# Quantised attention: who rounds the queries and keys of batches 2 to 7, and when

## What is computed

```python
def fake_quant(x, bits=8):
    qmax = 2.0 ** (bits - 1) - 1.0
    scale = jnp.maximum(jnp.max(jnp.abs(x)) / qmax, 1e-08)
    return jnp.clip(jnp.round(x / scale), -qmax - 1.0, qmax) * scale

qkv = fake_quant(x) @ fake_quant(w_qkv) + b_qkv
q, k, v = split_heads(qkv)                      # 12 heads of 16
attn = jnp.einsum('bhnd,bhmd->bhnm', fake_quant(q), fake_quant(k)) * scale
attn = fake_quant(jax.nn.softmax(attn, axis=-1))
out = jnp.einsum('bhnm,bhmd->bhnd', attn, fake_quant(v))
out = fake_quant(out) @ fake_quant(w_proj) + b_proj
```

## Time and profile before

| | us |
|---|---|
| median of 3 runs | 2291.52 (2283.61 to 2294.26) |
| the profiled execution, its own time | 2287.18 |
| its span, first to last instruction | 2285.4 |
| the rounding block, from the first to the last of its instructions | 819.2 to 853.7 |
| the first pass, first matmul to last exponential | 859.7 to 1118.5 |

### The profile page before, as it was taken

One profiled execution on the slowest core, in us unless ns is written; L12 is line 12 of the kernel. 1 busy time (PEld: TensorE's weight loads), 2 busy tenths in 40 slices (PEclk: granted clock), 3 DMA queues, 4 the chain that ended last, 5 costly groups with the idle time before them and its releaser, 6 DMA issues. The chain is left out here.

```text
span 2285.4 us, 30890 instructions
## 1 busy us (share of the span) xinstructions
PE 1875.7 (82%) x9852; PEld 972.1 (43%) x9876; DVE 1410.9 (62%) x2476; ACT 1140.9 (50%) x2071; POOL 458.9 (20%) x626
## 2 busy tenths in 40 slices
PE   5798899698875517777488877999899998999998
PEld 4644555354334201000122244442134334888887
DVE  6555255451105678999778887999788984223222
ACT  2044245341103759999799964332477770222222
POOL 6000000001211011222100013331024443333333
PEclk9989999777875755555599978996699999999999
DMA  3011111066991006432100009777788724676674
GB/s 89 14 55 65 60 33 35 5 249 237 410 411 50 0 4 197 133 106 95 33 29 28 28 16 151 125 125 105 81 98 114 109 56 141 171 212 200 199 211 105
DMA packets 153845, 262.04 MB, mean 115 GB/s; under 512 B 28640, under 2 KB 124497, under 8 KB 148726
## 3 DMA queue, kind: packets, MB, share of 16 engines
q1 hardware_dynamic: 135366, 242.23, 39.9%
q0 software_dynamic: 18256, 18.19, 4.0%
q10 hardware_dynamic: 96, 0.01, 0.0%
HBM read 217.80 MB, written 58.76 MB: 121 GB/s over the span
## 5 line engine op out<-in xcount | busy, mean ns | idle before, releaser
L1802 PE MATMUL ps<-arena 128*128 x376 | 194.8, 621 | 108.0 <-ACT ps L1844 60.2
L1844 ACT ACTIVATE ps<-ps,arena 128x512 f32<-128x512 f32 x384 | 256.6, 1120 | 6.4 <-POOL arena L1828 6.4
L1812 DVE TENSOR_REDUCE arena<-ps 128x1024 f32 x192 | 232.7, 1224 | 24.3 <-PE ps L1802 11.9
L1844 ACT ACTIVATION_READ_ACCUMULATOR ps<-ps,arena 128x1 f32 x384 | 234.7, 668 | 0.0
L2218 DVE TENSOR_REDUCE arena<-ps 128x1024 f32 x192 | 221.7, 1216 | 8.6 <-PE ps L2463 5.7
L2719 ACT ACTIVATE arena<-ps 128x1024 f32<-128x1024 f32 x192 | 185.3, 1021 | 77.1 <-PE ps L2571 75.4
L3060 ACT ACTIVATE arena<-ps,arena 128x256 f32<-128x256 f32 x234 | 89.5, 481 | 268.4 <-PE ps L3022 268.4
L2009 ACT ACTIVATE arena<-ps 128x1024 f32<-128x1024 f32 x192 | 178.7, 1048 | 7.9 <-DVE arena L2029 4.6
L2463 PE MATMUL ps<-arena 96*128 96x512 bf16 x500 | 164.0, 433 | 21.9 <-DVE arena L2218 12.1
L3091 DVE SCALAR_TENSOR_TENSOR arena<-ps,arena 128x192 f32<-128x192 f32 x78 | 29.0, 412 | 233.1 <-issue 233.1
L2992 POOL DMA_INDIRECT out_dram<-arena x78 | 121.3, 1555 | 238.1 <-DVE arena L3091 162.1
(11 more groups left out here) (413 smaller groups left out, 3347.8 us busy)
## 6 DMA issues: line engine op xcount, KB each, us to landing
arena<-in_sm_w_dram SPq DMA_DIRECT2D x128, 576.0 KB, 15.5
arena<-in_re_w_dram SPq DMA_DIRECT2D x39, 1252.0 KB, 5.8
arena<-ra_parts SPq DMA_DIRECT2D x192, 192.0 KB, 9.0
routed_in<-routed_in SPq DMA_DIRECT2D x8, 3332.0 KB, 13.6
ra_parts<-arena SPq DMA_DIRECT2D x48, 192.0 KB, 2.4
arena<-la_xt SPq DMA_DIRECT2D x16, 512.0 KB, 3.6
arena<-routed_in SPq DMA_DIRECT2D x39, 196.0 KB, 5.4
arena<-arena SPq DMA_DIRECT2D x64, 96.0 KB, 2.2
```

The source lines that it names most:

```text
L1802: ins = pe.matmul(ps[:, 2 * (n % 4) + t % 2, :], QM[j][:, h, t * P:(t + 1) * P], KI[:, b, h // HG, :], start=True, stop=True)
L1812: v.tensor_reduce(MXq[:, b, 2 * u:2 * u + 2, at_head(h)], ps[:, 2 * (n % 4):2 * (n % 4) + 2, :], AX.X, ALU.max).then_inc(s_lk, 1)
L1844: ins = act.activation(bank, bank, ACT.Exp, bias=nb[n % 4][:, t % 2:t % 2 + 1], scale=c_reg, accum_out=RS[:, b, t, at_head(h):at_head(h) + 1])
```

## The change

The loop over all batches in the rounding block goes; its body stays for batches 0 and 1, written out. The queries and keys of batches 2 to 7 are rounded by GpSimd within the first pass: in batch b it works on batch b+2, cut into 12 pieces of 128x512 (3 that scale and 3 that subtract, for the queries and then for the keys), one ahead of each odd unit's bias. In the last two batches, which have no b+2, it does the values of batches 0 and 1 instead, which neither ScalarE nor VectorE now touches: at units 3 and 9 a scaling of 128x384, at units 15 and 21 a memset and a subtraction of 128x384. SP waits for the rounded queries of a batch before it spreads them, TensorE for its rounded keys. `TA` are the two scratch tiles: the old `TMP` and one new.

```diff
         @block.scalar
             act.wait_ge(s_one, 16 * HG)
-            with act.Fori(0, B // 2) as i:
-                for n, (j, src, bias, k) in enumerate(((0, QF, magic, 0), (0, KF, magic_k, 1), (1, QF, magic, 0))):
...
-            rq.wait(act, B // 2, 0)
-            for b in range(2):
...
+            for n, (j, src, bias, k) in enumerate(((0, QF, magic, 0), (0, KF, magic_k, 1), (1, QF, magic, 0))):
+                if n == 2:
+                    rq.wait(act, 0, 1)
...
         @block.sync
                             sp.wait_ge(s_qz, 2)
+                            rounded[0].wait(sp, b, 3)
         @block.tensor
                     sg[j].wait(pe, i, 16 * HG)
+                    rounded[1].wait(pe, b, 3)
...
         @block.gpsimd
             nbs.start(pool)
+            for k in range(2):
+                pool.sem_inc(rounded[k].sem, 6)
+
+            def part(b, k, step):
+
+                some = slice(step % 3 * S, step % 3 * S + S)
+                if step < 3:
+                    if b > 2:
+                        rounded[k].wait(pool, b - 1, 3)
+                    pool.tensor_scalar(TA[k][:, some], scaled((QF, KF)[k], b)[:, some], inv2[:, k:k + 1],
+                                       (magic, magic_k)[k], ALU.mult, ALU.add).then_inc(scl_[k].sem, 1)
+                else:
+                    scl_[k].wait(pool, b - 2, 3)
+                    pool.tensor_scalar(scaled((QI, KI)[k], b)[:, some], TA[k][:, some], MAGIC, None,
+                                       ALU.subtract).then_inc(rounded[k].sem, 1)
+            def values(b, step):
+
+                heads = T * NH // 2
+                some = slice(step % 2 * heads * HD, (step % 2 + 1) * heads * HD)
...
+                if step < 2:
+                    if step == 0:
+                        rounded[b].wait(pool, B - 1, 3)
+                    pool.tensor_scalar(at, VF[:, b, :, :].rearrange("p t d -> p (t d)")[:, some], inv2[:, 2:3], magic,
+                                       ALU.mult, ALU.add).then_inc(s_va, 1)
+                else:
+                    pool.wait_ge(s_va, 2 * b + 2)
+                    pool.memset(VIb[:, :, HD:2 * HD], 0.0)
+                    pool.tensor_scalar(VIb[:, :, 0:HD], at.rearrange("p (h d) -> p h d", d=HD), MAGIC, None,
+                                       ALU.subtract).then_inc(s_vr, 1)
+
             for b in range(B):
                 for n in range(N1):
+                    if n % 2 and b + 2 < B:
+                        part(b + 2, n // 12, n // 2 % 6)
+                    elif n % 6 == 3 and b + 2 >= B:
+                        values(b + 2 - B, n // 6)
                     pool.wait_ge(s_lk, b * N1 + (n + 1))
                     ex.wait(pool, b, n - 3)
                     pool.tensor_scalar(nb[n % 4], MXq[:, b, 2 * (n % 2):2 * (n % 2) + 2, at_head(n // 2)], c_exp, -1.0,
```

More of the change, by code:

```diff
@@ L1710, in quantised_attention @@
     TM = [TMP] + [gt(P, [NG * S]) for _ in range(2)]
-    scaled = lambda src, b: src[:, bass.ds(b, 1), :, :].rearrange("p o x y -> p (o x y)")
+    scaled = lambda src, b: src[:, b, :, :].rearrange("p x y -> p (x y)")
     def round_v(v, b, rounded):
@@ L1722, in _ @@
             act.wait_ge(s_one, 16 * HG)
-            with act.Fori(0, B // 2) as i:
-                for n, (j, src, bias, k) in enumerate(((0, QF, magic, 0), (0, KF, magic_k, 1), (1, QF, magic, 0))):
[L1725 to L1730, removed]
-            rq.wait(act, B // 2, 0)
-            for b in range(2):
-                act.activation(TM[b][:, 0:T * D], VF[:, b, :, :].rearrange("p t d -> p (t d)"), ACT.Identity, bias=magic,
-                               scale=inv2[:, 2:3]).then_inc(s_vt, 1)
+            for n, (j, src, bias, k) in enumerate(((0, QF, magic, 0), (0, KF, magic_k, 1), (1, QF, magic, 0))):
+                if n == 2:
+                    rq.wait(act, 0, 1)
+                act.activation(TM[n % 2], scaled(src, j), ACT.Identity, bias=bias,
+                               scale=inv2[:, k:k + 1]).then_inc(tq.sem, 1)
         @block.vector
@@ L1739, in _ @@
             v.wait_ge(s_one, 16 * HG)
[L1740 to L1752, removed]
+            v.tensor_scalar(TM[2], scaled(KF, 1), inv2[:, 1:2], magic_k, ALU.mult, ALU.add).then_inc(s_kt, 1)
+            for n, (j, dst, k) in enumerate(((0, QI, 0), (0, KI, 1), (1, QI, 0), (1, KI, 1))):
+                if n < 3:
+                    tq.wait(v, 0, n + 1)
+                else:
+                    v.wait_ge(s_kt, 1)
+                v.tensor_scalar(scaled(dst, j), TM[n % 2 if n < 3 else 2], MAGIC, None, ALU.subtract
+                                ).then_inc(rq.sem, 1)
         @block.gpsimd
@@ L1772, in quantised_attention @@
     s_lk = sem("qa_pass1_chain")
+    rounded = [Signal(nc, f"qa_{n}_rounded_ahead", 3, 0) for n in "qk"]
+    scl_ = [Signal(nc, f"qa_{n}_scaled_ahead", 3, 0) for n in "qk"]
+    s_va, s_vr = sem("qa_v_scaled_ahead"), sem("qa_v_rounded_ahead")
+    TA = [TMP, g3(P, [NG * S])]
     with nc.Block(no_gpsimd_drain=True) as block:
@@ L1823, in _ @@
             nbs.start(pool)
+            for k in range(2):
[14 more added lines that the diff above has]
+                some = slice(step % 2 * heads * HD, (step % 2 + 1) * heads * HD)
+                at = TA[b][:, 0:T * D][:, some]
+                VIb = VI[:, b, :, :, :].rearrange("p t h d -> p (t h) d")[:, step % 2 * heads:(step % 2 + 1) * heads, :]
+                if step < 2:
[3 more added lines that the diff above has]
+                                       ALU.mult, ALU.add).then_inc(s_va, 1)
+                else:
+                    pool.wait_ge(s_va, 2 * b + 2)
+                    pool.memset(VIb[:, :, HD:2 * HD], 0.0)
+                    pool.tensor_scalar(VIb[:, :, 0:HD], at.rearrange("p (h d) -> p h d", d=HD), MAGIC, None,
+                                       ALU.subtract).then_inc(s_vr, 1)
             for b in range(B):
                 for n in range(N1):
+                    if n % 2 and b + 2 < B:
+                        part(b + 2, n // 12, n // 2 % 6)
+                    elif n % 6 == 3 and b + 2 >= B:
+                        values(b + 2 - B, n // 6)
                     pool.wait_ge(s_lk, b * N1 + (n + 1))
@@ L1889, in _ @@
             for b in range(2, B):
-                v.wait_ge(s_vt, b + 1)
+                v.wait_ge(s_vt, b - 1)
                 round_v(v, b, TV[:, b, :].rearrange("p (h d) -> p h d", d=HD))
```

## The result

| | before | after |
|---|---|---|
| median of the first comparison, 6 runs each | 2287.57 us (2281.46 to 2294.26) | 2255.35 us (2251.35 to 2260.32) |
| profiled execution: own time, span | 2287.18, 2285.4 us | 2256.84, 2255.1 us |
| all unchanged runs of this study | 2285.3 us median (80 runs, 2273.67 to 2296.03) | 2256.9 us median (17 runs, 2251.35 to 2266.01) |

The ratio of the first comparison is 0.9867, 95% interval 0.9848 to 0.9886: faster by 26 to 35 us. The forecast was 2265.5 us, 2258 to 2276. The sign was right, the measured time lies 2.7 us under the range. Of the 10 us between forecast and measurement, 1.8 are the starting point (2289.3 in the forecast, 2287.6 in this comparison), and 8.4 are a gain of 32.2 us where 23.8 was forecast.

A forecast was written before the change was run, and what follows sets the result against it. ScalarE was taken to pace the first pass, with the rounding block exposed ahead of it. 2287.2 - 23.8 + 0 = 2263.4 us; the median gave 2267.7; the middle, 2265.5, was forecast, range 2258 to 2276.

The forecast's parts named there:

- The rounding block: Block ahead of the first pass: three loop turns and the values of batches 0 and 1 leave, gaining 23.8 us.
- The new waits: SP's and TensorE's waits for rounded queries and keys in the first pass: cost 0.
- A piece: Each of 72 GpSimd pieces in the first pass: 0.7 us, upper bound 1.28, hidden, so cost 0.
- the room: GpSimd's time ahead of an odd unit's bias before ScalarE would miss it: 1.5 us ordinarily, 1.07 at unit 1.
- the 1.5: GpSimd's pieces in the first pass: the forecast called itself wrong if a piece takes over 1.5 us.
- A: Rival: pieces of 1.0 to 1.3 us hold up VectorE's addition at the batch's end, costing 1 to 6 us; chance 0.24.
- Rival B: First pass: pieces of 1.6 to 2.0 us outgrow the room, about 12 to 25 us, no measurable change; chance 0.05.
- Rival C: First pass: VectorE's maxima and GpSimd's pieces exclude each other, costing 37 us, so 2302, slower; chance 0.04.
- D: Rival: the rounding block before was not on the path, so the change misses; chance 0.03 with anything else.
- the sum's base: Whole kernel: starting time less 23.8 us, from the profiled 2287.2 us or the median, taking the middle, 2265.5.
- the range's low end: Whole kernel: fastest run before, 2283.6 us, less 23.8, 0.7 and 1 for the clock: 2258.

The follow-up runs named there:

- e7: Changed kernel with the piece of unit 21 moved to unit 23, where two subtracting pieces run one after the other; 2267.15 us, ratio 0.9923 to before.
- e6: Changed kernel with its 72 pieces in pairs ahead of every fourth unit instead of one ahead of every second; 2268.99 us, ratio 0.9953 to before.
- e5: Changed kernel with the subtracting piece written as a multiplication by 1 and an addition of -MAGIC; 2260.35 us, ratio 0.9892 to before.
- e10: Changed kernel, subtracting pieces in two forms: queries one operation with a column constant, keys two operations with constants in the instruction; 2263.15 us, one run.
- e1: The kernel before, unchanged, measured against itself; 2285.8 us, ratio 0.999.
- e4: Kernel before with 72 pieces of 128x512 added in the first pass on scratch alone, the rounding staying in its block; 2284.16 us, ratio 1.0002.
- e2: The changed kernel, unchanged, measured again; 2258.39 us, ratio 0.9876 to before.
- e3: Kernel before with the loop of the rounding block written out four times, all else as before; 2283.14 us, ratio 0.9989.
- e12: The changed kernel, unchanged, measured a third time; 2257.8 us, ratio 0.9897 to before.

## Why the prediction came out as it did

- **The rounding block, 23.8 us.** Right: 24.0 in the block itself, 23.7 up to the first matmul, the same in all three executions of each kernel.
- **The new waits, 0.** Right: pass 259.1 us in both.
- **A piece, 0.7 us.** The scaling piece was priced right (0.76). The subtracting one was mis-sized: 1.49, outside the bounds 0.7 to 1.28. Both ends came from rows of other instructions, and the form of the operation was taken as no matter. The wrong term is the slope: (1.49 - 0.27) / 512 = 2.4 ns a word for the single operation, not 0.82.
- **Why 1.49 us cost nothing all the same.** The subtracting pieces stand at units 7, 9, 11, 19, 21 and 23, where the room, read like the forecast's from the trace before, is 1.67, 1.56, 1.61, 1.50, 1.48 and 1.45 us. At unit 21 the piece just fits: the bias behind it has no idle time ahead of it, and ScalarE takes the unit at 923.41, 0.66 us after the exponential before, without a wait:

```profile
921.60 1.49 POOL L1831 TENSOR_SCALAR arena<-arena 128x512 bf16<-128x512 f32 x1
923.07 0.27 POOL L1859 TENSOR_SCALAR arena<-arena 128x2 f32<-128x2 f32 x1
```

```profile
922.75 1.30 ACT L1875 ACTIVATE ps<-ps,arena 128x512 f32<-128x512 f32 x1
923.41 1.31 ACT L1875 ACTIVATE ps<-ps,arena 128x512 f32<-128x512 f32 x1
```

  At unit 1 and the two odd units after it stand scaling pieces of 0.76. At unit 23 a piece was still running when the addition began, for which the forecast would have charged 0.6 us or more, and e7 shows that it doesn't hold the addition; bias 23 is held by the addition until 1.08 us after its start, before and after:

```profile
924.28 1.49 POOL L1831 TENSOR_SCALAR arena<-arena 128x512 bf16<-128x512 f32 x1
925.74 0.54 POOL L1859 TENSOR_SCALAR arena<-arena 128x2 f32<-128x2 f32 x1
```

```profile
925.20 0.95 DVE L1809 TENSOR_TENSOR arena<-arena 128x768 f32 x1
```

  Before, 956.66 - 955.58 = 1.08; after, 926.28 - 925.20 = 1.08. The forecast of no cost was right by luck, by two errors that cancelled: a piece too short, and an addition that waits for it. The piece was also only 0.01 us short of the 1.5 at which the forecast would have called itself wrong.
- **The rivals.** A's mechanism fell, and its price with it: the addition takes 0.95 us in the profile after too, where a piece is under way in six batches. Rival B's chain (1.5 us of room) is near the truth for an undisturbed pass, but e6 shows that the room grows to 2.3 us once ScalarE has waited, so its 12 to 25 us were probably too many; single pieces of 1.6 to 2.0 us were not run. Rival C fell: maxima 1.224 us in both. D fell: the shorter block came through whole.
- **The step that failed: the sum's base and the range's low end.** The sum let the time change by the block alone, from a base read off three runs, and the low end (the fastest of the three, 2283.6, less 23.8, 0.7 and 1 for the clock) gave everything outside the block 1 us. The runs showed in its place that equal code ahead of the block lasts 807.1 to 819.9 us, together with the granted clock, and that the kernel before goes from 2273.7 to 2296.0 us in 80 runs. In the first comparison the changed kernel's runs lay below their mean (2255.2 against 2257.1 over all 17) and those of the kernel before above theirs (2287.6 against 2285.0), so that the gain came out at 32 us; no run ties that excess to the change. Against the means of all runs, of the 8.4 us between forecast and 2257.1, 4.3 are the base (2289.3 for 2285.0), the block is 0.1 the other way, and about 4 stay unexplained.

## What to carry to other kernels

Price a change by the stretch in which the two kernels differ: 42.9 against 19.2 us repeated to a tenth, while whole executions of equal code spread over 22 us (compare the granted clocks before giving a difference outside that stretch a cause); and build a range from that spread, not from the extremes of three runs. Work cut to fit the gaps of an engine in a chain is free up to the room that the slowest engine's backlog leaves, and that room is read per unit, not from the engine's idle total (e6: 12 us idle per batch, and pairs of the same pieces cost 11 us over the pass). Before an instruction is moved to GpSimd, the form in which its arithmetic is written is worth a run of its own.

## What the runs showed of the hardware that was not expected

- GpSimd's TENSOR_SCALAR on 128x512 takes 1.49 us (constant in the instruction) or 1.57 (constant from a column) with one subtraction, and 0.62 to 0.76 with a multiplication and an addition (e5, e10, after).
- The exclusion between GpSimd and a VectorE addition with both inputs in SBUF is one-sided in these traces: a bias or a piece that begins while the addition runs is held (0.90 us instead of 0.27, 1.77 instead of 1.49), an addition that begins while a subtracting piece runs is not (0.95), nor is that piece (1.49). The Trainium skill, "SBUF — State Buffer", section "Who interferes with whom", says that such an addition contends with GpSimd's reads; another sentence there, on the 2-port modes, lets whoever issues first block the other for the whole instruction. Read onto the addition it would have held it here; the measurement decides.
- Between a memset of GpSimd and VectorE's 128x1536 TENSOR_SCALAR from SBUF to SBUF, the one that comes second waits for the first: 3.00 us for an instruction of 1.08, and 3.47 for a memset of 2.66 behind it. With two memsets in a row, either side can get the second turn: VectorE (before, e1, e4 to e7, e10) or the memset, though VectorE has waited longer (after, e2, e3, e12: 5.92 us). What decides isn't shown; the turn of the loop lasts 10.4 to 10.7 us either way.
